# One slot order, several moves: PV ahead of the next pair's first V products, with their copy and sum at the end of the slot

## The chip, the cores and the metric

The kernel runs on 1 core of one Trainium2 chip. The metric is the device time of one execution in microseconds. It was 1584.73 us in the median of 3 runs (1584.5 to 1585.61). PE is TensorE, ACT ScalarE, DVE VectorE, POOL GpSimd, SP the engine that issues most DMAs. A layer of a transformer is computed: gated cross-attention, then a gated feed-forward network with ternary weights.

## The reference, cut to what matters

```python
# x, ctx: (8, 1024, 512); w_q, w_k, w_v: (512, 512); W1: (2048, 512); W2: (512, 2048)
q = layernorm(x) @ w_q;  k = ctx @ w_k;  v = ctx @ w_v
scores = where(causal, q @ k.T / sqrt(512), -inf)
x = x + tanh(g_xattn[0]) * softmax(scores) @ v
h = gelu(layernorm(x) @ ternary(W1).T + b1)          # exact gelu
x = x + tanh(g_ffn[0]) * (h @ ternary(W2).T + b2)
# ternary(w) = clip(round(w / mean|w|), -1, 1)
```

## The kernel before, in words

**Numbers.** Every float32 operand of an attention product is split into two float16 parts, an upper one (written by ACT) and a lower one (the rest, written by DVE). A product is three passes: upper*upper, lower*upper, upper*lower. Queries and keys are not formed: with A = w_q w_k^T, the scores are T ctx^T with T = layernorm(x) A.

**Attention, slots 1 to 64.** The 8192 rows of x are 64 tiles of 128 rows, 8 tiles to a batch. A slot t handles one tile, and each engine has its own `slot` function whose statements are its queue, in program order; an engine never passes a waiting instruction. In slot t PE does: the scores of tile t (L1704, into `s_ps`, as wide as (t mod 8 + 1) * 128 columns), the T product of a later tile (`t_product`, L1663), V products, and PV of tile t-1 (L1751, into `o_ps`, 3 * (t mod 8) products for t mod 8 > 0, else 24). DVE masks the scores (L1200), takes the maximum (L1202), the layer-norm statistics of the row tile five slots ahead (L1211 to L1134), the lower part of P (L1222), of T (`t_lower`, L1163), the normalised rows (`ln_rows`, L1140), V parts, and the update of `x_ring` from `o_ps` (L1266). ACT does the exponential (L773), the upper parts of P (L778), T (L788) and the rows (`rows_upper`, L796). POOL takes the power -1/2 (L563) and the lower part of the rows (L567). SP turns P, rows and loads by DMA.

**V by seven products.** From the third batch on V is made by pairs of 128 context rows: 24 pairs, u = 0 to 23, with a Strassen-like scheme of seven half-size products, each six matmuls of 256 columns (L1606). Pair u is spread over three slots. In the odd slot t = 13 + 2u (`pre`) PE does products 1 and 2 (`v_pre`, `v_part` 1 into `vp_a`, 2 into `vp_b`), ACT copies product 1 into `vr[:, 0]` (`v_first`, L733, first of three counts of `vr_out` for this pair), and DVE adds product 2 to it (`v11`, L1077). In the even slot t = 14 + 2u (`main`) PE starts the slot with product 6 (`v_six`, which waits for `v_first` of this pair, since it adds to the bank that `v_first` copies), then the scores, then product 5 (`v_five`, which waits for ACT's copy L740, `v_second`), T, and products 7 and 3; ACT and DVE finish three blocks (L751, L758, L1083, L1095, L1103). In the odd slot t = 15 + 2u (`tail`) PE does product 4 (`v_four`), DVE adds it (`v21`, L1089), ACT takes the upper part (`v21_upper`, L764) and DVE the lower (`v21_lower`, L1111). So an odd slot is tail of one pair and pre of the next. `v_second` of the next pair waits for `v21_lower`.

**Order in an odd slot before.** PE: scores, T, `v_four`, `v_pre`, PV. ACT: exponential and P, `t_upper`, `v_first`, `rows_upper`, `v21_upper`. DVE: mask and statistics, P, `t_lower`, `ln_rows`, `v21`, `v11`, `v21_lower`, then ternary weights in some slots, then the `x_ring` update.

**Last slots.** Slots 57 to 62 also start the feed-forward stage: `y_stats` and `y_normal` (L1315 to L1319, L1333) for the first rows, POOL's sums (L621 to L626) and lower parts (`y_lower`, L632), which `y_normal` of a later row waits for, and in slots 61 and 62 four `weight_sums` of two operations each (L1307), which the first unit's products wait for (`w1_sums`).

**Feed-forward, 64 units U of four blocks.** Seven products of W1 (L1510), GELU on ACT (L909), lower parts on DVE (L1359), and W2 (L1568). `add_bias` on POOL (L641) adds b2 to the rows of x, four at a time, in the units named in `BIAS`; the last ternary weights (L1405 to L1408) are made in units 0 to 2 of DVE.

Of the kernel before, what the change touches and what calls it, by code (L numbers as in the profile page):

```python
# [18 lines left out]
def gated_block(nc, x, ctxT, g_xattn, g_ffn, wqT, wkT, wv, w1T, b1c, w2T, b2, out):  # L19
# [4 lines left out]
    NT = N // P  # L24
# [3 lines left out]
    GT = 4  # L28
    NG = NT // GT
# [19 lines left out]
    with es:  # L49
# [141 lines left out]
        w_negs, w_ternary = sem("w_negs"), sem("w_ternary")  # L191
# [126 lines left out]
        def x2_first(e):  # L318

            g, i = e // GT, TILE[e % GT]  # L320
            if g:
                return x2_at(g, i)
            return (X2_SPARE, g32[:, 1], x_ring[:, 0], x_ring[:, 1])[e]

        def rows_step(g):

            return 0 if g == 1 else 4 * g - 5
# [1 line left out]
        EARLY = 6  # L329
        ROWS_Q0 = {rows_step(g): g for g in range(2, NG)}  # L330
        ROWS_Q1 = {0: 1, **{rows_step(g) + 1: g for g in range(2, NG)}}
        BIAS = {rows_step(g) + 2: g for g in range(1, NG)}

        def t_bank(s):

# [205 lines left out]
        def _(pool):  # L541
# [93 lines left out]
            def add_bias(e):  # L635

                x2 = x2_at(e // GT, TILE[e % GT])
                pool.wait_ge(y_rows, e + 1)
                if e == 0:
                    pool.wait_ge(vp_mm[4], NP)  # L640
                g.tensor_tensor(x2, x2_first(e), b2_row[:, :], ALU.add).then_inc(x2_biased, 1)  # L641

            def last_sum(U):
# [30 lines left out]

            last_sum(0)
            y_lower(2)
            for e in range(GT):
                add_bias(e)
            for U in range(NU):
                if U in ROWS_Q0:  # L680
                    y_scale(ROWS_Q0[U] * GT)
# [16 lines left out]
        def _(act):  # L698
# [29 lines left out]
            def v_first(u):  # L728

                act.wait_ge(vp_mm[1], u + 1)  # L730
                if u:
                    act.wait_ge(vb_split, nth_of(u - 1, BD_DONE))
                a.activation(vr[:, 0], vp_a, ACT.Copy).then_inc(vr_out, 1)  # L733
# [69 lines left out]
            def slot(it, s, last=False):  # L803
                t = it * BODY + s
                split, pre, main, tail = pair(t, SPLIT_AT), pair(t, PRE_AT), pair(t, MAIN_AT), pair(t, LAST_AT)
                if last and t == NT - 1:
                    unit_copy(0)
                if pre is not None:
                    ctx_parts_upper(pre)
                if main is not None:  # L810
                    v_second(main)
                    v_third(main)
                if not last or t < NT:
                    softmax(it, s)
                if not last or t < NT - T_LEAD:
                    t_upper(it, s)
                if pre is not None and pre:
                    v_first(pre)
                if not last or t + LN_LEAD < NT:
                    rows_upper(it, s)  # L820
                if t == 1:
                    ctx_upper(0, 0, 3)
                for q in FIRST_SPLITS.get(t, ()):
                    ctx_upper(1, 1, q)
                if t == 4:
                    weight_parts_upper()
                if t + 1 < PLAIN * TB:
                    v_upper(it, s)
                if pre == 0:
                    v_first(pre)  # L830
                if tail is not None:
                    v21_upper(tail)
                if main is not None:
                    v12_upper(main)
                    vd_upper(main)
                if split is not None:
                    b, q, par = pair_at(split)
                    ctx_upper(b, par, q)
                for m, n in w_turn(t, "S"):
                    sum_weight(m, n)  # L840
                if last and t in (FIRST_Y + 2, FIRST_Y + 4, FIRST_Y + 6):
                    y_upper((t - FIRST_Y) // 2 - 1)
# [125 lines left out]
        def _(dve):  # L968
# [218 lines left out]
            def slot(it, s, last=False):  # L1187
# [25 lines left out]
                    ln_variance(k, rk)  # L1213
                if pre is not None:
                    ctx_parts_lower(pre)
                if y_row is not None:
                    y_stats(y_row)
                if last and t == NT - 1:
                    unit_copy(0)
                if live:  # L1220
                    dve.wait_ge(p_hi, t + 1)
                    v.scalar_tensor_tensor(out=p_s[:, r, LO, 0:(i + 1) * P], in0=p32[:, 0:(i + 1) * P], scalar=P_UP,  # L1222
                                           in1=p_s[:, r, HI, 0:(i + 1) * P], op0=ALU.mult,
                                           op1=ALU.subtract).then_inc(p_split, 1)
                if not last or t < NT - T_LEAD:
                    t_lower(it, s)
                if norm:
                    ln_rows(k, rk, src, s + LN_LEAD >= 2)
                if tail is not None:
                    v21(tail)  # L1230
                if pre is not None:
                    v11(pre)
                if tail is not None:
                    v21_lower(tail)
                if main is not None:
                    v22(main)
                    v12_lower(main)
                    vd_lower(main)
                if t in (5, 6):
                    weight_parts_lower(t - 5)  # L1240
                if t + 1 < PLAIN * TB:
# [2 lines left out]
                    ternary(m, n, w_in[:, m % WR], w_loaded[m % WR], 16 * (m // WR + 1))  # L1244
                if last and t == NT - 1:
                    unit_first(0)
                if last and t == NT - 3:
                    weight_sums(0)
                    weight_sums(1)
                if last and t == NT - 2:  # L1250
                    weight_sums(2)
                    weight_sums(3)
                if last and t == NT:
                    unit_second(0)
                    lower(0, 0)
                if s >= 1:

                    q = (s - 1) % 2
                    v.reciprocal(rinv[:, q:q + 1], rowsum[:, q:q + 1]).then_inc(o_inv, 1)
                    dve.wait_ge(o_inv, t)  # L1260
                    par = ((s - 1) // TB) % 2
                    v.tensor_scalar(osc[:, q:q + 1], rinv[:, q:q + 1], fsc[:, par:par + 1], None,
                                    ALU.mult).then_inc(o_scaled, 1)
                    dve.wait_ge(o_scaled, t)
                    dve.wait_ge(pv_mm, t + PV0)
                    v.scalar_tensor_tensor(out=x_ring[:, (s - 1) % 8], in0=o_bank(last, s), scalar=osc[:, q:q + 1],  # L1266
                                           in1=x_ring[:, (s - 1) % 8], op0=ALU.mult, op1=ALU.add).then_inc(o_done, 1)
                if t == 1:
                    ctx_lower(0, 0, 3)
                for q in FIRST_SPLITS.get(t, ()):  # L1270
# [10 lines left out]
                if split is not None:  # L1281
                    b, q, par = pair_at(split)
                    ctx_lower(b, par, q)
                if y_row is not None:
                    y_normal(y_row)
                if t in TOTAL_SLOTS:
# [200 lines left out]
        def _(pe):  # L1487
# [198 lines left out]
            def slot(it, s, last=False):  # L1686
# [30 lines left out]
                    v_four(tail)  # L1717
                if t == PRE_AT:
                    v_product(it, s)
                if pre is not None:  # L1720
                    v_pre(pre)
                if last and t == NT:

                    unit_second(0)
# [10 lines left out]
                if s >= 1:  # L1735
# [13 lines left out]
                    for n, (pa, va) in enumerate(PASSES):  # L1749
                        for j in range(jn + 1):  # L1750
                            last_mm = mm(o_bank(last, s), pT[:, (s - 1) % 2, pa, j], v_s[:, par, va, j],  # L1751
                                         start=(n == 0 and j == 0), stop=(n == 2 and j == jn))
                    last_mm.then_inc(pv_mm, 1)

            pe.wait_ge(consts, 1)
            for _ in range(WARM):
# [75 lines left out]
```

## Time and profile before

| | |
|---|---|
| median of 3 runs | 1584.73 us |
| the profiled execution | 1584.63 us |
| its span, from first to last instruction | 1582.8 us |
| PE busy | 1554.9 us (98%) |
| DVE / ACT / POOL busy | 1165.2 / 871.8 / 590.3 us |
| granted PE clock over the span | 0.998 |

The span is what the trace covers; 1.83 us lie around it. A row of the timeline gives start and duration in us, engine, source line, operation, output and inputs, how many instructions were merged, and in brackets the idle time before it and who ended it. A row of the groups gives busy time, mean ns of one, and the idle time before them. Matmuls are pipelined: a product of 256 columns lasts 273 ns in the records, while six of them follow each other in 0.65 us, so the end of a merged PE row overlaps the next.

### The profile page before, as it was taken

The numbers are of one execution on the slowest core, as the hardware profiler recorded it, in microseconds if no ns is written. First come the engines' busy times: TensorE is split into PE (matmuls) and PEld (weight loads), VectorE is DVE, ScalarE is ACT, GpSimd is POOL, SyncE is SP. The second block draws the span as 40 slices with busy tenths as digits, with TensorE's granted clock in tenths as the row PEclk, the third lists the DMA queues.
The fourth block names the chain that finished last, engine by engine and source line by source line (L and its number), as shares of the span: only waits on it lengthen the run. The fifth ranks groups of instructions, "written<-read, shape, count | busy, mean of one in ns | idle before, by whom it ended". The sixth has DMA issues, their size and how long they took to land.

```text
span 1582.8 us, 27584 instructions
## 1 busy us (share of the span) xinstructions
PE 1554.9 (98%) x10456; PEld 1019.6 (64%) x10456; DVE 1165.2 (74%) x1973; ACT 871.8 (55%) x1575; POOL 590.3 (37%) x569
## 2 busy tenths in 40 slices
PE   8899999999999999998999999999999999999998
PEld 4556666676766666664666666666666666666665
DVE  6776678788988888876877667766766676767664
ACT  4344445544445444444666666666666666666654
POOL 5311223333324333243444444334534453445330
PEclk9999999999999999999999999999999999999999
DMA  7558657765656655553522333323332242224210
GB/s 213 140 104 196 149 139 185 150 145 137 146 132 144 150 130 132 134 141 85 127 77 78 66 82 82 83 72 65 93 83 78 49 101 77 77 48 100 51 51 27
DMA packets 310996, 170.91 MB, mean 108 GB/s; under 512 B 268544, under 2 KB 268560, under 8 KB 310608
## 3 DMA queue, kind: packets, MB, share of 16 engines
q1 hardware_dynamic: 309392, 166.52, 43.6%
q10 hardware_dynamic: 1296, 2.36, 0.4%
q8 instruction: 83, 1.36, 0.3%
q14 instruction: 49, 0.40, 0.1%
q0 software_dynamic: 176, 0.27, 0.1%
HBM read 70.53 MB, written 33.55 MB: 66 GB/s over the span
## 4 chain that ended last, share of the span: by engine, by line
PE 72%; DVE 16%; ACT 5%; issue 4%; DMA 1%; POOL 0%; SPq 0%; DVEq 0%; ACTq 0%
PE s_ps L1568 14%; PE e_ps L1568 13%; PE t_ps L1510 7%; PE v_ps L1510 7%; PE o_ps L1510 7%; PE o_ps L1751 6%; PE s_ps L1704 5%; PE t_ps L1663 5%; PE m_ps L1510 3%; PE e_ps L1606 2%; PE v_ps L1682 2%; DVE negmax L1202 2%; DVE ctx_s L989 2%; DVE x_ring L1266 1%; DVE xn_both L1140 1%
## 5 line engine op out<-in xcount | busy, mean ns | idle before, releaser
L1359 DVE SCALAR_TENSOR_TENSOR v_s<-xnT,sc,v_s 128x512 f16<-128x512 f32 x256 | 239.5, 956 | 105.7 <-ACT v_s L916 105.7
L909 ACT ACTIVATE xnT<-tT,b_s 128x256 f32<-128x256 f32 x384 | 174.0, 500 | 180.9 <-DVE tT L1347 64.8
L1568 PE MATMUL s_ps<-raw,v_s 128*128 128x512 f16 x1024 | 262.8, 379 | 0.8 <-DVE raw L1408 0.8
L1568 PE MATMUL e_ps<-raw,v_s 128*128 128x512 f16 x1024 | 262.8, 379 | 0.0
L1704 PE MATMUL s_ps<-ctx_s,tT 128*128 128x512 f16 (+3 forms) x1152 | 197.7, 326 | 4.7 <-DVE tT L1163 3.9
L1751 PE MATMUL o_ps<-v_s,pT 128*128 128x512 f16 x840 | 193.3, 381 | 3.5 <-DVE x_ring L1266 3.5
L916 ACT ACTIVATE v_s<-xnT,sc 128x512 f16<-128x512 f32 x256 | 176.2, 712 | 8.1 <-ACT xnT L909 0.8
L1568 PEld LDWEIGHTS e_ps<-raw,v_s 128*128 128x128 f16 x1024 | 100.2, 98 | 120.8
L647 POOL TENSOR_TENSOR tT<-tT 128x512 f32<-128x512 f32 x64 | 81.1, 1268 | 247.7 <-ACT tT L936 247.7
L1663 PE MATMUL t_ps<-xnT,a_s 128*128 128x256 f16 x1488 | 172.7, 273 | 0.1
L1704 PEld LDWEIGHTS s_ps<-ctx_s,tT 128*128 128x128 f16 x1152 | 105.5, 98 | 92.5 <-DVE tT L1163 5.9
L563 POOL TENSOR_TENSOR rstd<-var_s,minus_half 128x1 f32<-128x1 f32 x61 | 56.0, 919 | 291.7 <-DVE var_s L1134 291.7
L773 ACT ACTIVATE p<-s_ps,ebias,esc 128x128 f32<-128x128 f32 (+3 forms) x64 | 53.2, 831 | 194.4 <-DVE ebias L1206 194.4
L1663 PEld LDWEIGHTS t_ps<-xnT,a_s 128*128 128x128 f16 x1488 | 145.3, 98 | 21.0 <-DMA xnT<-xn_both 0.3
L1568 PEld LDWEIGHTS s_ps<-raw,v_s 128*128 128x128 f16 x1024 | 100.1, 98 | 68.1 <-issue 1.1
L1751 PEld LDWEIGHTS o_ps<-v_s,pT 128*128 128x128 f16 x840 | 82.5, 98 | 93.6 <-issue 6.1
L567 POOL TENSOR_TENSOR xn_both<-xn_both 128x512 f16<-128x512 f32 x61 | 71.1, 1166 | 150.0 <-ACT xn_both L796 150.0
L615 POOL TENSOR_TENSOR rstd<-var_s,minus_half 128x1 f32<-128x1 f32 x64 | 36.1, 565 | 218.8 <-DVE var_s L1319 218.8
L1341 DVE COPY tT<-t_ps 128x512 f32<-128x512 f32 x64 | 44.2, 691 | 85.0 <-PE t_ps L1510 85.0
L796 ACT ACTIVATE xn_both<-xn_both 128x512 f16<-128x512 f32 x64 | 40.3, 630 | 90.5 <-DVE xn_both L1140 90.0
L1353 DVE TENSOR_TENSOR tT<-tT,t_ps 128x512 f32<-128x512 f32 x64 | 44.0, 688 | 50.3 <-ACT tT L930 26.3
L641 POOL TENSOR_TENSOR v_work<-v_work,b_row 128x512 f32<-128x512 f32 x40 | 75.4, 1913 | 0.0
(232 smaller groups left out, 2831.2 us busy)
## 6 DMA issues: line engine op xcount, KB each, us to landing
out_y<-x_ring SPq DMA_DIRECT2D x128, 256.0 KB, 2.2
x_ring<-in_x SPq DMA_DIRECT2D x63, 256.0 KB, 2.9
raw<-in_ctxT SPq DMA_DIRECT2D x28, 512.0 KB, 4.0
v_work<-out_y SPq DMA_DIRECT2D x40, 256.0 KB, 3.9
w_in<-in_w1T SPq DMA_DIRECT2D x16, 512.0 KB, 3.8
w_in<-in_w2T SPq DMA_DIRECT2D x12, 512.0 KB, 3.9
x_ring<-out_y SPq DMA_DIRECT2D x22, 256.0 KB, 3.8
xnT<-xn_both SPq DMA_TRANSPOSE x128, 2.6
```

The costliest lines, as they stand in the source:

```text
L563: g.tensor_tensor(rstd[:, r:r + 1], var_s[:, r:r + 1], minus_half[:, :], ALU.pow).then_inc(ln_rstd, 1)
L567: g.tensor_tensor(xn_s[:, r, LO], xn32[:, r], xn_s[:, r, HI], ALU.subtract).then_inc(xn_lo, 1)
L641: g.tensor_tensor(x2, x2_first(e), b2_row[:, :], ALU.add).then_inc(x2_biased, 1)
L647: g.tensor_tensor(rr[:, R3], rr[:, R3], rr[:, R5], ALU.add).then_inc(c22_sum, 1)
L909: a.activation(g32n[:, j, half * 2 * P:(half + 1) * 2 * P], src, ACT.Gelu, bias=b1_s[:, f:f + 1], scale=1.0 / YN).then_inc(g_act, 1)
L916: a.activation(g_s[:, U % 2, j, HI], g32n[:, j], ACT.Copy, scale=col(C_SG)).then_inc(g_hi, 1)
L1359: v.scalar_tensor_tensor(out=g_s[:, U % 2, j, LO], in0=g32n[:, j], scalar=col(C_SG), in1=g_s[:, U % 2, j, HI], op0=ALU.mult, op1=ALU.subtr ...
L1510: last_mm = mm(bank[:, p * 2 * P:(p + 1) * 2 * P], w, yT[g % 2][:, a, row, c, :], start=(first and p == 0 and a == HI and c == 0), stop=(a ...
L1568: last_mm = mm(y_ps[i], g_s[:, U % 2, j, a, i * P:(i + 1) * P], w2_s[:, f, :], start=(U % UG == 0 and n == 0 and a == HI), stop=(U % UG == ...
L1663: last_mm = mm(bank[:, dd], a_s[:, aa, c, d * P:(d + 1) * P], xnT[:, pr, xa, c, :], start=(n == 0 and c == 0), stop=(n == 2 and c == DC - 1))
L1704: last_mm = mm(s_ps[:, lo:hi], tT[:, pr, ta, c, q * P:(q + 1) * P], ctx_s[:, par, ca, c, lo:hi], start=(n == 0 and c == 0), stop=(n == 2 a ...
L1751: last_mm = mm(o_bank(last, s), pT[:, (s - 1) % 2, pa, j], v_s[:, par, va, j], start=(n == 0 and j == 0), stop=(n == 2 and j == jn))
```

## The change

Nothing is computed otherwise; statements change their place in the queues. PE: `v_pre` goes behind PV. ACT: in the odd slot `v21_upper` goes ahead of `rows_upper`, and `v_first` to the end, behind `rows_upper` and (in even slots only) the context parts. DVE: `v21` goes ahead of `ln_rows`, `v11` behind the `x_ring` update; `y_stats` goes behind the V parts; the four `weight_sums` go from slots 61 (0, 1) and 62 (2, 3) to slot 62 (0, 1 in their old place, 2 behind the update) and slot 63 (3). POOL: the first four `add_bias` go from ahead of unit 0 to unit 2 and wait for the last ternary weights; those of group 1 go from unit 2 to unit 4.

```diff
@@ BIAS
-        BIAS = {rows_step(g) + 2: g for g in range(1, NG)}
+        BIAS = {2: 0, 4: 1, **{rows_step(g) + 2: g for g in range(2, NG)}}
@@ POOL, add_bias
                 if e == 0:
                     pool.wait_ge(vp_mm[4], NP)
+                    pool.wait_ge(w_ternary, NW)
@@ POOL, behind the slots
             y_lower(2)
-            for e in range(GT):
-                add_bias(e)
             for U in range(NU):
@@ ACT, slot
                     t_upper(it, s)
-                if pre is not None and pre:
-                    v_first(pre)
+                if tail is not None:
+                    v21_upper(tail)
                 if not last or t + LN_LEAD < NT:
                     rows_upper(it, s)
...
-                if pre == 0:
-                    v_first(pre)
-                if tail is not None:
-                    v21_upper(tail)
                 if main is not None:
                     v12_upper(main)
                     vd_upper(main)
                 if split is not None:
                     b, q, par = pair_at(split)
                     ctx_upper(b, par, q)
+                if pre is not None:
+                    v_first(pre)
@@ DVE, slot
-                if y_row is not None:
-                    y_stats(y_row)
                 if last and t == NT - 1:
                     unit_copy(0)
+                    weight_sums(3)
...
                     t_lower(it, s)
+                if tail is not None:
+                    v21(tail)
                 if norm:
                     ln_rows(k, rk, src, s + LN_LEAD >= 2)
-                if tail is not None:
-                    v21(tail)
-                if pre is not None:
-                    v11(pre)
                 if tail is not None:
                     v21_lower(tail)
                 if main is not None:
                     v22(main)
                     v12_lower(main)
                     vd_lower(main)
+                if y_row is not None:
+                    y_stats(y_row)
...
-                if last and t == NT - 3:
+                if last and t == NT - 2:
                     weight_sums(0)
                     weight_sums(1)
-                if last and t == NT - 2:
-                    weight_sums(2)
-                    weight_sums(3)
...
                                            in1=x_ring[:, (s - 1) % 8], op0=ALU.mult, op1=ALU.add).then_inc(o_done, 1)
+                if pre is not None:
+                    v11(pre)
...
                     ctx_lower(b, par, q)
+                if last and t == NT - 2:
+                    weight_sums(2)
                 if y_row is not None:
                     y_normal(y_row)
@@ PE, slot
-                if pre is not None:
-                    v_pre(pre)
...
                     last_mm.then_inc(pv_mm, 1)
+                if pre is not None:
+                    v_pre(pre)
```

## Rows read from the trace of the kernel before

**Rows 1.** Busy time in the pairs' slots; PE, PEld, DVE, ACT, POOL, clock, DMA.
```profile
187.00:691.00 504.00, 499.69 (x3541) 340.07 (x3538) 425.10 (x842) 233.35 (x433) 176.29 (x187) 1.00 0.60 142
```

**Rows 2.** Groups of PE instructions: products 6 and 5 of all pairs.
```profile
L1606 PE MATMUL e_ps<-v_work 128*128 128x256 f16 x432 | 59.0, 273 | 4.3 <-ACT vr L740 4.0
```

**Rows 3.** Timeline of slot 41 and the start of 42, odd-slot work.
```profile
...
496.35 0.38 ACT L733 ACTIVATE vr<-e_ps 128x256 f32<-128x256 f32 x1 [0.62 <-PE e_ps L1606]
...
496.56 0.68 DVE L1163 SCALAR_TENSOR_TENSOR tT<-t_ps,tT 128x512 f16<-128x512 f32 x1
...
497.16 0.54 DVE L1140 TENSOR_SCALAR xn_both<-x_ring,mv,rstd 128x512 f32<-128x512 f32 x1
...
497.45 0.82 PE L1606 MATMUL e_ps<-v_work 128*128 128x256 f16 x6
497.62 0.41 DVE L1089 TENSOR_TENSOR vr<-vr,e_ps 128x256 f32<-128x256 f32 x1
497.73 0.63 ACT L796 ACTIVATE xn_both<-xn_both 128x512 f16<-128x512 f32 x1 [1.00 <-DVE xn_both L1140]
...
498.70 1.17 DVE L1111 SCALAR_TENSOR_TENSOR v_s<-vr,v_s 128x256 f16<-128x256 f32 x1 [0.34 <-ACT v_s L764]
```

**Rows 4.** Timeline: the same two points of slots 43, 45 and 47.
```profile
514.83 0.68 DVE L1163 SCALAR_TENSOR_TENSOR tT<-t_ps,tT 128x512 f16<-128x512 f32 x1
...
515.41 0.82 PE L1606 MATMUL e_ps<-v_work 128*128 128x256 f16 x6
...
537.69 0.68 DVE L1163 SCALAR_TENSOR_TENSOR tT<-t_ps,tT 128x512 f16<-128x512 f32 x1
...
538.45 0.82 PE L1606 MATMUL e_ps<-v_work 128*128 128x256 f16 x6
...
564.71 0.68 DVE L1163 SCALAR_TENSOR_TENSOR tT<-t_ps,tT 128x512 f16<-128x512 f32 x1
...
566.41 0.82 PE L1606 MATMUL e_ps<-v_work 128*128 128x256 f16 x6
```

**Rows 5.** Timeline: end of T on PE, t_lower on DVE, slots 40, 42, 44.
```profile
484.42 0.82 PE L1606 MATMUL e_ps<-v_work 128*128 128x256 f16 x6
...
485.25 0.69 DVE L1163 SCALAR_TENSOR_TENSOR tT<-t_ps,tT 128x512 f16<-128x512 f32 x1 [0.38 <-ACT tT L788]
...
503.69 0.82 PE L1606 MATMUL e_ps<-v_work 128*128 128x256 f16 x6
...
505.03 0.69 DVE L1163 SCALAR_TENSOR_TENSOR tT<-t_ps,tT 128x512 f16<-128x512 f32 x1
...
522.61 0.39 PE L1577 MATMUL m_ps<-g,ones 128*128 128x128 f32 x2
...
524.86 0.68 DVE L1163 SCALAR_TENSOR_TENSOR tT<-t_ps,tT 128x512 f16<-128x512 f32 x1
```

**Rows 6.** Timeline of slots 61 to 64.
```profile
714.54 1.29 DVE L1307 TENSOR_TENSOR wv_s<-w_s 128x1024 f16<-128x1024 f16 x2
715.75 4.67 DVE L1307 TENSOR_TENSOR wv_s<-wv_s,w_s 128x1024 f16<-128x1024 f16 x2
715.83 4.03 POOL L632 TENSOR_TENSOR v_s<-v_s 128x1792 f16<-128x1792 f32 x1 [3.99 <-ACT v_s L860]
...
721.67 5.73 PE L1751 MATMUL o_ps<-v_s,pT 128*128 128x512 f16 x18 [3.51 <-DVE x_ring L1266]
...
732.62 0.30 DVE L1200 TENSOR_TENSOR s_ps<-s_ps,causal 128x128 f32<-128x128 f32 x1 [1.76 <-PE s_ps L1704]
...
742.78 5.35 PE L1751 MATMUL e_ps<-v_s,pT 128*128 128x512 f16 x24 [0.43 <-DMA pT<-p_s]
```

**Rows 7.** Timeline of the feed-forward units 1 and 2.
```profile
768.65 1.05 PE L1510 MATMUL t_ps<-ctx_s,a_s 128*128 128x256 f16 x8 [1.38 <-DVE tT L1341]
...
787.31 6.75 POOL L641 TENSOR_TENSOR v_work<-v_work,b_row 128x512 f32<-128x512 f32 x4
...
793.08 1.02 PE L1568 MATMUL s_ps<-raw,v_s 128*128 128x512 f16 x4 [0.82 <-DVE raw L1408]
```

## The prediction

> **What bounds the kernel now.** I read the busy times by stretch first. In the pairs' slots PE is busy 499.69 of 504 us [rows 1], and DVE 425: PE sets the pace, with DVE close behind, so what counts is each wait of PE. Then I read who ended PE's waits. In those slots the only ones of weight are product 5's waits for ACT's copy L740, 4.3 us of idle time [rows 2]; they stand in nine slots. The records hide part of each: a product of 256 columns lasts 273 ns [rows 2], but six follow each other in 0.65 us, so 0.16 of its record overlaps the next. The nine waits cost 4.3 + 9*0.16 = 5.8 us. Behind the pairs come a wait of 3.51 for DVE's `x_ring` update in slot 62 and one of 0.43 for P's DMA in slot 64 [rows 6], and 1.38 and 0.82 in units 1 and 2 [rows 7]. Nearly every us that an edit adds on PE's own path is a us of the kernel; one that it takes from DVE is worth something only at these waits.
>
> **What the reordering does to an odd slot.** Last I read the timeline of one odd slot and the start of the next [rows 3]. PE reaches product 6 at 497.45. ACT copied product 1 at 496.35, well before. The row copy L796 ran from 497.73 to 498.36, after PE had started product 6. Now L733 is put behind L796 on ACT, which never overtakes. So product 6, which needs L733, waits for a chain that nothing of PE waited for before. Moving `v_pre` behind PV leaves PE's arrival at product 6 where it was (the same work stands before it), and takes away the PV that lay between product 1 and product 6.
>
> The new chain, counted from the start of `t_lower`: L1163 to the next 0.60 (496.56 to 497.16), `v21` now first, with the 0.33 by which L1077 follows L1089 (0.41 busy, less the overlap of 0.08), rows L1140 0.54, hand-over 0.03 (497.70 to 497.73), row copy L796 0.63 less an overlap of 0.10 between neighbours on ACT, copy L733 0.38, hand-over to PE 0.06. Together 2.47 us. `v21_upper` fits beside the rows.
>
> Held against PE's arrival, if DVE kept its place:
> - slot 41: 496.56 + 2.47 = 499.03 against 497.45, 1.58 late [rows 3];
> - slot 43: 517.30 against 515.41, 1.89 late [rows 4];
> - slot 45: 540.16 against 538.45, 1.71 late [rows 4];
> - slot 47: 567.18 against 566.41, 0.77 late [rows 4].
> These four repeat in every batch.
>
> **What DVE gains back.** `v21_lower` L1111 took 1.17 and had 0.34 of idle time before it [rows 3]. It will start before POOL's work on the rows instead of beside it, and its ACT half will be ready: I take 0.42 and no wait, near the 0.41 of L1089, which has the same 256 columns (bounds 0.41 and 1.17). That is 1.1 us of DVE per odd slot, and PE comes later besides, so in the even slot DVE masks in time. There `t_lower` can't come sooner than T: 0.83 after T's end in slot 40 (484.42 to 485.25), where nothing held it. In slot 42 it came after 1.34, in slot 44 after 2.25 [rows 5]. So at most 0, 0.51 and 1.42 are won before slots 41, 43 and 45, and the rest of the even slot's DVE work follows as before. Slot 47 has a wider slot before it, with more DVE lateness to win; I take all of its 0.77.
>
> The waits at product 6: 1.58 in slots 17, 25, ... 57 (6 times, 9.5), 1.89 - 0.51 = 1.38 in slots 19, 27, ... 51 (5 times, 6.9), 1.71 - 1.42 = 0.3 in slots 21 ... 53 (5 times, 1.5), none in slots 23 ... 55. Sum 17.9. Bounds: with another 1.1 off each they sum to 6*0.48 + 5*0.28 = 4.3; no gain of DVE at all gives 6*1.58 + 5*1.89 + 5*1.71 + 5*0.77 = 31.3.
>
> On the other side all of the 5.8 at product 5 goes: `v21_lower`, which L740 waited for, ends over 1 us sooner, and PE comes later. Bounds 4 and 5.8. Net in the pairs' slots +12.1.
>
> **Slots 59 to 64.** Slot 59 has no row copy, but `v_first` stands behind `v21_upper`; its wait delays PE against a DVE that is late there anyway, so it is not added. The wait of 3.51 in slot 62 goes: no `weight_sums` stand before the update of slot 61. With it goes a slower stretch: 18 products took 5.73 where, at the (5.35 - 0.16)/24 = 0.216 of slot 64's, 18*0.216 + 0.16 = 4.05 would do [rows 6], 1.7 more. Worth 5.4. But who is late next? The second pair of L1307 took 4.67, the first 1.29, because POOL's L632, 4.03 long, lay across it [rows 6]. Now `y_normal` stands where that pair stood, and POOL's lower part comes no sooner, since it is queued behind a power that waits for the moved `y_stats`. I take DVE to be held till it ends, so that slot 62's mask comes about when it did. Ahead of the last mask DVE had 1.76 of idle time, so it was ready at 730.9 [rows 6]. Slot 62 now carries one pair of L1307 more, 1.3, and `y_stats`, which had stood in the shadow of ACT's P and now follows P: no row here, between 0.7 (one operation over 512 columns, as L1163's 0.68 [rows 3]) and 1.3; I take 1.0. The mask comes at 733.2, though PE has its scores 5.2 sooner, near 727.5. From that mask to the last PV, 732.62 to 742.78, is 10.16 [rows 6], a chain of DVE, ACT and DMA that PE's lead can't shorten: 743.4. So the last PV comes 0.6 later than it did, the wait moves from slot 62 to slot 64, 4 us or more, and the slow stretch behind a wait of that length comes again. I take +2.3 for this part (0.6 and 1.7). Bounds: -6.0, if DVE is held nowhere and the gain is kept (5.4, and 0.43 + 0.16 in slot 64), and +4.
>
> In the Trainium skill, SBUF — State Buffer, section Who interferes with whom, a VectorE operation with two SBUF inputs, or one in a 2-port mode as `tensor_scalar` may be, is fully blocked behind a GpSimd operation that reads SBUF. By that rule `y_normal` is held as the L1307 pair was, and the trace agrees for L1307 (4.67 beside 4.03). Were only two-input operations held, this part would give the lower bound.
>
> **Units 0 to 4.** Four `add_bias` ahead of unit 0 no longer lie beside DVE's work, and I take the 1.38 + 0.16 of unit 1 to go with them [rows 7]. Unit 2's 0.82 + 0.16 ends with a ternary operation beside POOL's 6.75 us of adds [rows 7]; the adds now wait for it. Gain 2.5. Bounds: 2.5, and a loss of 1 if the adds of units 2 and 4 hold DVE elsewhere. In slots 1 to 16 and from unit 5 on nothing on PE's path changes; the later groups of `add_bias` stand as they did.
>
> **Sum.** Against the profiled execution's 1584.63 (span 1582.8 and 1.83 around it, 0.1 below the median of 1584.73): +17.9 - 5.8 + 2.3 - 2.5 = +11.9, 1596.5.
>
> **Rivals.**
> *The tail keeps its gain.* DVE is not held in slot 61, the last mask is on time: -6.0 instead of +2.3, 1588.2. For it: DVE had 1.76 of idle time before that mask. Against it: the amount of work moved there.
> *Faster: DVE's lead is carried through.* The 1.1 us per odd slot that L1111 and its wait give back comes off the chain of the next odd slot in full. The waits at product 6 sum to 4.3, which the 5.8 at product 5 pays; with the tail's 6.0 and the units' 2.5 the time is 1574.6. It decides once the waits at product 6 sum to less than 14.3 with the tail kept. Against it: in slot 40 `t_lower` followed T as soon as it could [rows 5], so there is nothing to be won before slot 41.
> *The late copy doesn't bind.* PE doesn't wait at product 6 at all, since the rows are done by then: -5.8 + 2.3 - 2.5, 1578.6. Against it: L796 ended 0.9 after product 6 had started [rows 3].
> *DVE wins nothing for the odd slots.* Another operation meets POOL's work in place of L1111, and masks stay as late as before: +31.3 - 5.8 + 2.3 - 2.5, 1609.9.
>
> **How the numbers follow.** Forecast 0.64, within 1591 to 1601; the tail's gain kept 0.12; DVE's lead 0.07; copy not binding 0.03; nothing won 0.12; 0.02 for neither. About 0.2% (3.2 us) is what a measurement of this kernel tells from no change. The tail rival straddles that bound: half same, half slower. So faster 0.1, same 0.07, slower 0.83. The range runs from the tail rival's lower half to midway to the worst case: 1585 to 1603.
>
> **What would show it.** Right: PE waits at L1606 for L733, some 17 times, 1.4 to 1.6 in slots 1 and 3 of a batch; L740 is gone as its releaser; L1111 falls to 0.4; the largest single PE wait is at the last PV, for pT, and none for the `x_ring` update; no PE wait in units 1 and 2. Wrong: PE's idle time in the pairs' slots stays under 8 us, or the last mask follows the last scores at once.

## The result and the profile after

The changed kernel took 1596.23 us in the median (1594.69 to 1597.79), the one before 1584.63 (1584.5 to 1585.61) beside it: the ratio is 1.0072, interval 1.0057 to 1.0088. The change makes the kernel slower by 0.72%, 11.6 us; the forecast was +11.9.

The page of the profile after. Its execution was the longest one, 1597.79 us, so 1.6 over the median:

```profile
span 1596.0 us, 27584 instructions
PE 1557.7 (98%) x10456; PEld 1019.2 (64%) x10456; DVE 1150.5 (72%) x1973; ACT 874.6 (55%) x1575; POOL 586.2 (37%) x569
```

DVE gave back 14.7 us of work, and the span still grew by 13.2. The busy times of the pairs' slots, the same stretch as [rows 1] (columns: stretch, its length, then PE, weight loads, DVE, ACT, POOL, granted clock, DMA share, GB/s):

```profile
187.00:691.00 504.00, 489.25 (x3453) 330.44 (x3452) 400.68 (x820) 230.92 (x424) 167.37 (x181) 1.00 0.61 140
```

PE's idle time grew from 4.3 to 14.75 us at an unchanged clock. The chief waits of PE by who ended them (total, times, longest):

```profile
PE e_ps L1603 <- ACT vr L732: 16.4, 17, 1.7
PE s_ps L1492 <- DMA ctx_s<-in_wqT: 3.4, 2, 2.6
PE e_ps L1660 <- DMA xnT<-xn_both: 3.4, 1, 3.4
PE s_ps L1701 <- DVE tT L1160: 2.9, 3, 1.9
PE v_ps L1507 <- ACT tT L927: 2.4, 1, 2.4
PE s_ps L1701 <- ACT p L772: 1.8, 2, 1.0
```

And the groups that answer to [rows 2] (L1606 is L1603 now) and to the 1.17 of L1111 in [rows 3] (the second is the view of that line by itself: min, median and longest duration in ns):

```profile
L1603 PE MATMUL e_ps<-v_work 128*128 128x256 f16 x432 | 59.1, 273 | 16.4 <-ACT vr L732 16.4
```
```profile
L1108 DVE SCALAR_TENSOR_TENSOR v_s<-vr,v_s x24: 424/425/426, 218.8 to 729.7; 128x256 f16<-128x256 f32 x24
```

Product 5's wait for ACT's second copy is gone, and 17 waits for the first copy (L732, L733 before) stand in its place. One of them step by step, the end of slot 41 and the start of slot 42, against [rows 3]:

```profile
504.36 0.82 PE L1603 MATMUL e_ps<-v_work,ctx_s 128*128 128x256 f16 x6
505.01 0.81 PE L1746 MATMUL o_ps<-v_s,pT 128*128 128x512 f16 x3
505.66 0.82 PE L1603 MATMUL e_ps<-wv_s,ctx_s 128*128 128x256 f16 x6
506.08 0.68 DVE L1160 SCALAR_TENSOR_TENSOR tT<-t_ps,tT 128x512 f16<-128x512 f32 x1
506.31 0.82 PE L1603 MATMUL v_ps<-wv_s,ctx_s 128*128 128x256 f16 x6
506.68 0.41 DVE L1086 TENSOR_TENSOR vr<-vr,e_ps 128x256 f32<-128x256 f32 x1
507.01 0.54 DVE L1137 TENSOR_SCALAR xn_both<-x_ring,mv,rstd 128x512 f32<-128x512 f32 x1
507.12 0.42 ACT L763 ACTIVATE v_s<-vr 128x256 f16<-128x256 f32 x1 [1.87 <-DVE vr L1086]
507.57 0.42 DVE L1108 SCALAR_TENSOR_TENSOR v_s<-vr,v_s 128x256 f16<-128x256 f32 x1
507.58 0.63 ACT L795 ACTIVATE xn_both<-xn_both 128x512 f16<-128x512 f32 x1
508.12 0.37 ACT L732 ACTIVATE vr<-e_ps 128x256 f32<-128x256 f32 x1
508.29 1.16 POOL L567 TENSOR_TENSOR xn_both<-xn_both 128x512 f16<-128x512 f32 x1 [2.06 <-ACT xn_both L795]
508.54 0.83 PE L1603 MATMUL e_ps<-v_work 128*128 128x256 f16 x6 [1.41 <-ACT vr L732]
```

Read it from the bottom. PE starts product 6 at 508.54, when the copy at 508.12 is done. The copy stood behind the rows' copy (507.58) on ACT, that behind `ln_rows` on DVE (507.01), that behind `v21` (506.68) and `t_lower` (506.08). Yet ACT had been idle for 1.87 us ahead of 507.12, and the product that it copies ended with the six products of 505.66. PE waits for a queue's order, not for data or for work.

The last slots, against [rows 6] (the first row is where slot 60's scores start):

```profile
707.59 3.42 PE L1701 MATMUL s_ps<-ctx_s,tT 128*128 128x512 f16 x24
...
731.75 3.59 POOL L632 TENSOR_TENSOR v_s<-v_s 128x1792 f16<-128x1792 f32 x1
732.17 3.44 DVE L1330 TENSOR_SCALAR w_in<-v_work,mv,rstd 128x512 f32<-128x512 f32 x1
735.54 0.29 DVE L1197 TENSOR_TENSOR s_ps<-s_ps,causal 128x128 f32<-128x128 f32 x1
738.57 5.34 PE L1701 MATMUL s_ps<-ctx_s,tT 128*128 128x512 f16 x24 [1.01 <-ACT p L772]
...
746.65 0.29 DVE L1197 TENSOR_TENSOR s_ps<-s_ps,causal 128x128 f32<-128x128 f32 x1
...
752.47 1.28 ACT L906 ACT_TABLE_LOAD   x1
755.21 1.05 PE L1507 MATMUL v_ps<-ctx_s,a_s 128*128 128x256 f16 x8 [2.40 <-ACT tT L927]
756.81 6.82 PE L1746 MATMUL e_ps<-v_s,pT 128*128 128x512 f16 x24 [0.55 <-DMA pT<-p_s]
```

`y_normal` (L1330) is held for 3.44 us beside POOL's 3.59; one such operation that is held nowhere takes 0.54, as L1137 above. In the program this `y_normal` waits for no count of that lower part, so it isn't a semaphore that holds it. The wait of 3.51 for `x_ring` is gone. In the stretch behind 756.7 the granted clock falls to 0.61, as it fell to 0.57 behind the wait of 3.51 before:

```profile
756.70:760.70 4.00, 3.89 (x12) 1.50 (x13) 1.04 (x3) 2.79 (x6) 2.58 (x2) 0.61 0.02 7
```

### The profile page after: what moved, and what is told of

Read it like the earlier page. It is cut to its first block, busy times and chain, and to the rows that moved or that the text cites. A ratio compares the mean times of both kernels' runs of the same rounds, so it can differ in the third digit from the quotient of the medians.

```text
span 1596.0 us, 27584 instructions
## 1 busy us (share of the span) xinstructions
PE 1557.7 (98%) x10456; PEld 1019.2 (64%) x10456; DVE 1150.5 (72%) x1973; ACT 874.6 (55%) x1575; POOL 586.2 (37%) x569
## 3 DMA queue, kind: packets, MB, share of 16 engines
q8 instruction: 83, 1.36, 0.4%
## 4 chain that ended last, share of the span: by engine, by line
PE 76%; DVE 14%; ACT 4%; issue 3%; DMA 1%; POOL 1%; SPq 0%; DVEq 0%; ACTq 0%
PE s_ps L1565 14%; PE e_ps L1565 14%; PE s_ps L1701 7%; PE o_ps L1507 7%; PE t_ps L1507 7%; PE v_ps L1507 7%; PE o_ps L1746 6%; PE t_ps L1660 5%; PE m_ps L1507 3%; PE e_ps L1603 3%; PE v_ps L1679 2%; DVE ctx_s L986 2%; DVE negmax L1199 1%; DVE v_work L1065 1%; DVE x_ring L1259 1%
## 5 line engine op out<-in xcount | busy, mean ns | idle before, releaser
L1603 PE MATMUL e_ps<-v_work 128*128 128x256 f16 x432 | 59.1, 273 | 16.4 <-ACT vr L732 16.4
```

The source lines that it names most:

```text
L1603: last_mm = mm(bank, left(ca, c), right(va, c), start=(first and n == 0 and c == 0), stop=(n == 2 and c == 1), skip_group_check=True)
```

## Experiments

Each ratio is against the kernel before, run on the same chip in the same rounds (its medians were 1585.29, 1585.95 and 1585.39 in the three groups of runs), with its 95% interval. Two theories stood against each other. Theory A: the late place of `v_first` on ACT makes PE wait, and the other moves help or are nothing. Theory B: PV's place ahead of `v_pre`, or the moves of the last slots, cost the time.

### The copy early, the products ahead of PV, and each part by itself

**e1_copy_early**, the change with one call moved on ACT:

```diff
                     t_upper(it, s)
+                if pre is not None:
+                    v_first(pre)
                 if tail is not None:
                     v21_upper(tail)
...
-                if pre is not None:
-                    v_first(pre)
                 for m, n in w_turn(t, "S"):
```

> The changed kernel with one statement moved: ACT's copy of product 1 stands directly behind the upper part of T, ahead of v21_upper and of the row copy; PV stays ahead of products 1 and 2. My theory (product 6 waits only because its copy is queued behind the rows, which wait for DVE): the 17 waits at product 6, 19.2 us in the changed kernel's profile, fall under 2 us in all, since the copy needs 0.38 and product 2 runs 0.65 beside it. The product-5 waits of the old kernel don't come back, since v21_lower stays early. Time 1596.2 - 17.5 = 1578.7, within 1577 to 1581, and faster than the kernel before. Rival A (the nearness of product 1 to product 6, now that PV no longer lies between them, is what costs): a wait of 0.4 or more stays in each of 23 slots, and the rows come later behind a copy that waits for PV: 1588 or more. Rival B (the rest of the change, DVE's order or the last slots, carries the loss): 1594 or more.

1579.22 us (1578.0 to 1580.18), ratio 0.9961 [0.9948, 0.9973]. One call's place turns the change from 0.7% slower to 0.4% faster, 17 us. In its trace, the same group and the same stretch as above:

```profile
L1603 PE MATMUL e_ps<-v_work 128*128 128x256 f16 x432 | 59.0, 273 | 1.5 <-ACT vr L739 1.3 <-ACT vr L732 0.3
187.00:691.00 504.00, 502.49 (x3564) 340.96 (x3563) 412.74 (x850) 238.24 (x441) 175.11 (x190) 1.00 0.61 143
```

The 16.4 us are 0.3, and PE is idle for 1.51 of 504 us. Against the expectation, 1.3 us of product 5's waits (for L739) came back, in two slots.

**e2_products_before_pv**, the change with PE's move undone:

```diff
                     v_product(it, s)
+                if pre is not None:
+                    v_pre(pre)
                 if last and t == NT:
...
                     last_mm.then_inc(pv_mm, 1)
-                if pre is not None:
-                    v_pre(pre)
```

> The changed kernel with PE's move undone: products 1 and 2 stand ahead of PV again, ACT and DVE as changed. My theory: the wait at product 6 ends with the copy behind the rows, whose chain starts at t_lower; PE's order inside the slot changes neither that chain nor PE's arrival at product 6. So the waits stay at 19 us, 1.5 in slots 1 and 1.4 in slots 3 of a batch, and the time at 1596 (1594.5 to 1598). Rival A (the place of PV): the waits go, 1578 to 1582.

1595.78 (1594.15 to 1596.2), 1.0064 [1.0052, 1.0077]: no different from the change. The waits didn't move either:

```profile
PE e_ps L1603 <- ACT vr L732: 16.5, 17, 1.7
```

PV's place costs nothing here, and theory B's first half falls. The traces say it more sharply than the times: from slot 0's first score product to the last product of the program the change takes 1548.94 us and e2 1549.01. It also shows that product 1 is early enough in either place.

**e3_only_copy_late**, the kernel before with the late copy alone:

```diff
                     t_upper(it, s)
-                if pre is not None and pre:
-                    v_first(pre)
                 if not last or t + LN_LEAD < NT:
                     rows_upper(it, s)
...
-                if pre == 0:
+                if pre is not None:
                     v_first(pre)
                 if tail is not None:
                     v21_upper(tail)
```

> The kernel before with one statement moved: ACT's copy of product 1 stands behind the row copy, ahead of v21_upper. My theory: the chain from t_lower to product 6 is 2.47 less the 0.33 of v21, 2.14 us, so product 6 is late by 1.25 in slots 1 and by 1.56 less 0.5 in slots 3 of a batch, and by about 0.2 in slots 5: 6*1.25 + 5*1.1 + 5*0.2 = 14. Product 5 waits less, but not in the narrow first slot of a batch, since DVE's v11 now waits for the copy ahead of v21_lower: 2 of its 5.8 go. Time 1584.6 + 14 - 2 = 1596.6, within 1592 to 1600: this one move alone costs what the whole change costs. Rival B (the loss comes from DVE's order, PE's order or the last slots): 1583.5 to 1587.

1593.26 (1591.05 to 1594.89), 1.0051 [1.0038, 1.0065]. One move by itself costs 8 us. It came out 3.3 below the value expected, though inside the range: the waits in slots 1 and 3 of a batch are shorter than I had them (slot 1: 1.11 to 1.24), apart from slot 57's 2.19, slot 5 has none, and all of product 5's went. So a PE that comes later is enough to hide product 5's copy, with `v21_lower` as late as before.

```profile
PE e_ps L1604 <- ACT vr L733: 11.3, 11, 2.0
```

11.3 and 11 * 0.17 hidden in the records make 13.2, less the 5.8 of product 5: 7.4. A wait for T in slot 60, 0.66 and its hidden part, went with them: 6.6, and the two traces differ by 6.5 from slot 0's first score product on. The change has the longer waits since there `v21` comes ahead of `ln_rows` too: the 0.33 that the prediction counted for it is the difference in each of ten slots (1.44 to 1.57 in slot 1 of a batch, against 1.11 to 1.24 here).

**e10_copy_between**, the change with the copy halfway, behind `v21_upper` and ahead of `rows_upper`:

```diff
                     v21_upper(tail)
+                if pre is not None:
+                    v_first(pre)
                 if not last or t + LN_LEAD < NT:
...
-                if pre is not None:
-                    v_first(pre)
```

> The changed kernel with ACT's copy of product 1 between v21_upper and the row copy. My theory gives the length of the chain for this place as well: from the start of t_lower 0.60, v21 0.41, hand-over 0.04, v21_upper 0.40 less 0.10, copy 0.38, hand-over 0.06, together 1.79 instead of 2.47, 0.68 shorter. So the 17 waits of 1.5, 1.35 and 0.33 become about 0.85 six times, 0.65 five times and none, 1.2 in slot 59: 9.5 less than in the changed kernel, 1596.2 - 9.5 = 1586.7, within 1585 to 1589, halfway to the early copy's 1579.2. Rival D (it is the row copy as such that holds ACT, so anything ahead of it is free): 1579 to 1581.

1587.43 (1584.32 to 1589.69), 1.0012 [1.0003, 1.0021].

```profile
PE e_ps L1603 <- ACT vr L732: 8.3, 12, 1.7
```

Behind the rows 1596.23, ahead of them 1587.43, ahead of `v21_upper` as well 1579.22: the time follows the copy's place step by step. Slot 1 of a batch waits 0.77 to 0.91 here and slot 3 0.56 to 0.71, as the chain with the rows' terms taken off gives. Slot 59 still waits 1.88, where 1.2 was expected: no row copy stands in it, so this move changes nothing there. No run came near rival D's 1579 to 1581 (the fastest took 1584.32). Theory A stands.

**e15_only_third_block_early**, the kernel before with only the third block moved, the copy staying first:

```diff
@@ ACT
                     v_first(pre)
+                if tail is not None:
+                    v21_upper(tail)
                 if not last or t + LN_LEAD < NT:
...
-                if tail is not None:
-                    v21_upper(tail)
@@ DVE
                     t_lower(it, s)
-                if norm:
-                    ln_rows(k, rk, src, s + LN_LEAD >= 2)
                 if tail is not None:
                     v21(tail)
+                if norm:
+                    ln_rows(k, rk, src, s + LN_LEAD >= 2)
```

> The kernel before with v21 ahead of ln_rows on DVE and v21_upper ahead of the row copy on ACT, v_first staying ahead of both: the part of the change that I take to be its gain. My theory: v21_lower runs before POOL's rows work, 0.42 instead of 1.17, and the nine waits at product 5, 5.8 us, go down to 0 to 1; nothing waits at product 6; the last slots keep their waits. 1585.5 - 5.3 = 1580.2, within 1579 to 1582. Rival (that time is given back at the next wait, DVE being close behind): 1584 or more.

1581.37 (1577.51 to 1582.74), 0.9972 [0.996, 0.9983]. This is the part of the change that pays in the pairs' slots. L1111 takes 0.42 in all 24 slots, and of product 5's 4.3 us nothing is left; the 0.3 is a wait at product 6 in slot 57:

```profile
L1606 PE MATMUL e_ps<-v_work 128*128 128x256 f16 x432 | 58.9, 273 | 0.3 <-ACT vr L733 0.3
```

### The last slots and the units

**e4_last_slots_undone**, the change with `y_stats` and the `weight_sums` back in their old places:

```diff
+                if y_row is not None:
+                    y_stats(y_row)
                 if last and t == NT - 1:
                     unit_copy(0)
-                    weight_sums(3)
...
-                if y_row is not None:
-                    y_stats(y_row)
...
-                if last and t == NT - 2:
+                if last and t == NT - 3:
                     weight_sums(0)
                     weight_sums(1)
+                if last and t == NT - 2:
+                    weight_sums(2)
+                    weight_sums(3)
...
-                if last and t == NT - 2:
-                    weight_sums(2)
```

> The changed kernel with y_stats and the four weight_sums in their old places. My theory: the wait of 3.5 us for the x_ring update in slot 62 and its slow stretch come back and the waits in slot 64 go, since the last mask is the same chain either way; y_stats ahead of P costs 1 us at product 6 in slot 57. Net between -1 and +2, 1596.8. Rival (those moves keep their gain of 5.4, and something else in the last slots costs): 1601 or more.

1593.23 (1592.77 to 1596.95), 1.0057 [1.0044, 1.007]. That is 2.0 below the lower end of what was expected. By the ratios the moves of the last slots cost 0.15% in the change, 2.4 us, but the intervals of the two overlap. In the trace the `x_ring` wait is back, and this time no slow stretch follows it: 18 products took 5.73 there before [rows 6] and take 4.04 here. Nor does one follow the wait of 0.41 at the last PV. But one stands earlier: slot 57's wait at product 6 is 2.35, 1.0 longer than in the change, as expected of `y_stats`, and behind it the granted clock of 4 us is 0.57.

```profile
686.67 0.99 PE L1603 MATMUL e_ps<-v_work 128*128 128x256 f16 x6 [2.35 <-ACT vr L732]
...
736.73 4.04 PE L1746 MATMUL o_ps<-v_s,pT 128*128 128x512 f16 x18 [2.88 <-DVE x_ring L1261]
...
756.13 5.35 PE L1746 MATMUL e_ps<-v_s,pT 128*128 128x512 f16 x24 [0.41 <-DMA pT<-p_s]
```
```profile
687.00:691.00 4.00, 4.00 (x18) 2.10 (x16) 1.50 (x3) 0.38 (x1) 3.92 (x6) 0.57 0.43 116
```

So of what the change removed and brought back, 1.7 us and 1.5 are the clock behind a wait, which is not at the same wait in every trace. From slot 0's first score product on, e4's trace is only 0.4 us shorter than the change's; that the moves of the last slots cost anything is not shown.

**e11_early_row_late**, e1 with slot 61's `y_normal` put behind the next slot's mask:

```diff
                                     ALU.mult).then_inc(s_bias, 1)
+                if y_row == 5:
+                    y_normal(4)
                 if norm:
...
-                if y_row is not None:
+                if y_row is not None and y_row != 4:
                     y_normal(y_row)
```

> The kernel with the early copy (1579.2 us), and DVE's normalising of the fifth feed-forward row moved from the end of slot 61 behind the mask and bias of slot 62. My theory: that operation is what lies 3.44 us behind POOL's lower part and makes the mask of slot 62 about 1.9 late; the mask reads PSUM and isn't held by POOL. Moved behind it, the wait of 1.2 for the exponential in slot 63 goes, and the chain to the last PV starts up to 1.8 sooner: 1577.4, within 1576.5 to 1579. Rival (the last PV is set by POOL's and ACT's rows work anyway): 1579.2.

1577.7 (1575.84 to 1578.86), 0.9948 [0.9936, 0.9961], which overlaps e1's interval. The order of DVE beside POOL's lower part:

```profile
714.74 3.59 POOL L632 TENSOR_TENSOR v_s<-v_s 128x1792 f16<-128x1792 f32 x1
716.70 0.30 DVE L1197 TENSOR_TENSOR s_ps<-s_ps,causal 128x128 f32<-128x128 f32 x1 [1.46 <-PE s_ps L1703]
717.03 1.09 DVE L1199 TENSOR_REDUCE negmax<-s_ps 128x1 f32<-128x896 f32 x1
718.29 0.54 DVE L1332 TENSOR_SCALAR w_in<-v_work,mv,rstd 128x512 f32<-128x512 f32 x1
```

The mask and the maximum, which read PSUM, run at their usual length in the middle of POOL's operation; `y_normal` now starts as that operation ends (718.29 against 718.33) and takes 0.54 instead of 3.44. PE's wait of 1.0 for the exponential is gone. From slot 60's scores to the end of the last PV the trace is 2.8 us shorter than e1's: 1.1 are waits, and 1.7 a fall of the clock that e1's trace has and this one has not.

**e12_early_row_late_stats_early**, e11 with `y_stats` back ahead of P's lower part:

```diff
                     ctx_parts_lower(pre)
+                if y_row is not None:
+                    y_stats(y_row)
...
-                if y_row is not None:
-                    y_stats(y_row)
```

> As the one before, and y_stats back ahead of P's lower part, where DVE waits for ACT in slots 60 to 62. My theory: 1.0 us of DVE goes back into that shadow in each of slots 60, 61 and 62, and the last mask, late against PE's scores, comes 1 sooner in slot 62; in slots 57 to 59 it stands ahead of P and can cost up to 1. Net 0 to -1 against it: 1576.8, within 1575.5 to 1578. Rival (y_stats ahead of P costs more in slots 57 to 59 than it gives): 1578.5 or more.

1576.06 (1575.09 to 1577.58), 0.9938 [0.9925, 0.9952]. It lies in the range expected, but its interval overlaps e11's. In the traces it loses 1.1 us against e11 up to slot 60's scores and wins 2.4 from there to the end of the last PV.

**e9_early_bias_undone**, e1 with the `add_bias` moves undone:

```diff
-        BIAS = {2: 0, 4: 1, **{rows_step(g) + 2: g for g in range(2, NG)}}
+        BIAS = {rows_step(g) + 2: g for g in range(1, NG)}
...
-                    pool.wait_ge(w_ternary, NW)
...
             y_lower(2)
+            for e in range(GT):
+                add_bias(e)
```

> The kernel with the early copy (1579.2 us), and the adds of b2 back ahead of unit 0 and in unit 2. My theory: the waits of 1.5 for DVE's copy in unit 1 and of 1.0 for the ternary weights in unit 2 come back, 2.3 net of the 0.25 that is left now: 1581.5, within 1580.5 to 1582.5. Rival (DVE catches up there, the waits are paid back later): 1579.

1580.35 (1579.63 to 1582.8), 0.9968 [0.9956, 0.9981], against 0.9961 of e1, and just below the range expected. The waits of units 1 and 2 are back in the trace (1.32 and 0.98 with the hidden parts, against 0.25 in the change), but in time only 1.1 us shows, inside both intervals. That these moves win 2 us rests on the traces, not on a timed difference.

### The best version

**e6_early_products_before_pv** is e1 with `v_pre` ahead of PV again, **e13_best_products_before_pv** is e12 with the same edit:

```diff
                     v_product(it, s)
+                if pre is not None:
+                    v_pre(pre)
...
-                if pre is not None:
-                    v_pre(pre)
```

> The kernel with ACT's copy of product 1 directly behind the upper part of T (1579.2 us), and besides that products 1 and 2 ahead of PV again. My theory: once the copy is early, PV's place is off PE's path: products 1 and 2 and PV take the same time in either order, and the 0.38 of the copy is hidden beside product 2 or beside PV. Same time, 1578 to 1580.5. Rival A (PV ahead costs something by itself, the copy and its hand-over just behind product 1): faster by 2 or more, under 1577. Rival C (PV ahead is what frees DVE's x_ring update and so pays): 1582 or more.

1577.85 (1577.12 to 1579.57), 0.9951 [0.9938, 0.9963]. With the copy early neither product 5 nor product 6 waits any more, and PE fills the whole stretch:

```profile
L1603 PE MATMUL e_ps<-v_work 128*128 128x256 f16 x432 | 58.9, 273 | 0.0
187.00:691.00 504.00, 504.00 (x3578) 343.66 (x3576) 414.09 (x853) 237.56 (x439) 175.82 (x191) 1.00 0.62 143
```

The 0.10% to e1 is within both intervals, so the times alone don't tell the two apart. The traces do: from slot 0's first score product to slot 60's, e6 takes 645.91 us and e1 647.97. The 2.06 are e1's two waits for L739 and the one for L732, with their hidden parts. So beside the early copy `v_pre` ahead of PV is worth 2 us in the trace, while beside the late copy (e2) it was worth nothing. The expectation had it off PE's path.

> The fastest kernel so far (1576.1: early copy, fifth row behind the mask, y_stats ahead of P) with products 1 and 2 ahead of PV again. My theory: as beside the early copy alone, where it was 1577.9 against 1579.2 and the last waits at products 5 and 6 (2.1 us) were gone from the profile: 1574.5, within 1573 to 1576. Rival (that difference was scatter): 1576.

1574.59 (1572.99 to 1574.77), 0.9929 [0.9917, 0.9941]: the fastest here, 0.7% ahead of the kernel before and 1.4% ahead of the change. The interval overlaps e12's again, and the traces again give 2.0 us up to slot 60's scores (647.20 against 649.23). It keeps of the change the third block ahead of the rows, `v11` behind the update, the spread `weight_sums` and the late `add_bias`, and has `v_first` and `y_stats` early.

## Why the prediction was right

The time (1596.23 against 1596.5) and the cause are as predicted, and so is the sign; two terms were off against each other: slot 59's wait, left out, and the last slots, put too high. The traces sum to 10 where I had 11.9, so the mechanism is shown, but a forecast within 0.3 us of the median is luck. Durations below are from starts to starts, with the part that the records hide.

- **The chain.** 2.47 us were counted from `t_lower` to product 6. In slot 41 it is 506.08 to 508.54, 2.46.
- **The waits at product 6.** Slot 1 of a batch: 1.44 to 1.57 against 1.58, 9.1 in all against 9.5. Slot 3: 1.22 to 1.36 against 1.38, 6.6 against 6.9. Slot 5: 0.33 five times, 1.65 against 1.5. Slot 7: none, as said. Sum 17.4 against 17.9. That DVE's gain reaches back only as far as T lets it, the argument on slots 40, 42 and 44 [rows 5], is what sized these; with no gain it would have been 31.3.
- **Product 5.** All 5.8 gone. Both reasons given hold: `v21_lower` ends sooner (L1108 took 0.42, the value taken), and PE comes later; by e15 and e3 either is enough alone.
- **Slot 59.** I left its wait out, as delaying PE against a DVE that is late anyway. It is 1.87 us.
- **Slots 60 to 64.** `y_normal` is held behind POOL, the mechanism forecast. The Trainium skill, SBUF — State Buffer, section Who interferes with whom, names `tensor_scalar` as an operation that can block on GpSimd; by that rule, the trace agrees (3.44 against 3.59). It says as well that an operation with one SBUF input outside those modes doesn't contend, and the mask and maximum from PSUM in e11 agree. From slot 60's scores to the last PV PE loses 6.5 us in the changed kernel against 7.6 before; with slot 59 it is 8.4. So +0.8 stands where I had +2.3. What I mis-sized is the mask of slot 62, which I took to come when it did: it comes 2.1 us sooner, 27.95 behind slot 60's scores against 30.09 (the rows below, and 735.54 against 707.59 above). DVE's update of `x_ring` now starts ahead of POOL's operation (L1259 at 731.51 against 731.75), where before it came behind it (L1266 at 720.77, POOL's end at 719.86). The detail was wrong too: I had the one large wait at the last PV, for pT. The last mask came at 746.65 and the last PV 10.16 later, to the hundredth as before; but the 4 us of waiting fell apart into 0.53, 1.17, 2.57 and 0.72 at four places. The largest is at a product ahead of the last PV, which needs a bank that ACT copies (L927) behind P, a copy of rows, a table load of 1.28 and the first GELU. It would have been seen by asking, for each product of PE in the last slot, whose bank it overwrites.
- **Units 0 to 4.** 2.3 gained in the trace, 2.5 forecast.

The start of slot 60's scores and the mask of slot 62 in the kernel before:

```profile
691.80 3.43 PE L1704 MATMUL s_ps<-ctx_s,tT 128*128 128x512 f16 x24 [0.66 <-DVE tT L1163]
...
721.89 0.29 DVE L1200 TENSOR_TENSOR s_ps<-s_ps,causal 128x128 f32<-128x128 f32 x1
```

By the traces this sums to 17.4 - 5.8 + 0.8 - 2.3 = +10.1. The profiled execution came out 13.16 above the one before, and 3.25 of it lie ahead of slot 0's first score product, where no edit is (the first row is of the kernel before, the second of the changed one):

```profile
39.35 0.83 PE L1704 MATMUL s_ps<-ctx_s,tT 128*128 128x128 f16 x12
```
```profile
42.60 0.83 PE L1701 MATMUL s_ps<-ctx_s,tT 128*128 128x128 f16 x12
```

PE waits 3.4 there for the first weights (L1492, 0.8 before); in e2's trace, of the same head, that wait is 0.2. From this product to the last one of the program the traces differ by 9.94, so the account leaves nothing open between them. The medians are 11.6 apart, 1.6 more. Each trace is one execution: over the 13 traces the head ends between 39.16 and 42.60, and each fall of the clock behind a wait adds about 1.5 us or more. The 34 executions of the kernel before beside the experiments have medians of 1585.29 to 1585.95, and from these the change is 10.3 to 10.9 away. Why e4's waits from slot 61 on cost 3.6 us where those of the change cost 5.0 stays open; these are single traces of each.

The rivals: that the late copy doesn't bind fell by e1 and e10. That DVE wins nothing for the odd slots fell with slot 3 and slot 5 of the batches. That DVE's lead is carried through fell, since it can't pass T. That the tail keeps its gain fell as stated, +0.8 instead of -6.0.

## What to carry to other kernels

On an in-order engine the copy that frees or fills a bank for the bottleneck engine belongs where its input is ready, ahead of anything that waits for a slower chain: here its place alone, with the same work, was worth 17 us, 1.1%. Size such a wait by adding the chain from the last point that can't move, and let a lead won upstream count only as far as that point lets it. Bundled moves are to be timed one by one: one of these lost 17 us beside the others (8 by itself) and hid others that, without it, win 6. And a move that was worth nothing beside a wait (`v_pre` in e2) can be worth something once that wait is gone (2 us in e6's trace).

## What was not expected of the hardware

- Behind PE's wait of 3.51 [rows 6] and behind 2.40 and 0.55 in a row in the change, the granted clock fell to 0.57 and 0.61 of the 4 us that follow, near the lower of its two levels (1.2 against 2.4 GHz) for some 3 us, which cost 1.7 and 1.5 us. The last PV's 24 products took 6.82 for it, against 5.35 in e4. Behind e4's wait of 2.88 it stayed at full speed, though it fell behind the 2.35 of slot 57 in the same trace. In e15 the fall behind 3.51 lasted longer: the 18 products took 6.89, 2.8 us more than the 4.05 of the change. The clearest case is the scores of slot 62, where e1 and e6 both waited 2.00 for T: in e6 the clock fell and the 24 products took 1.7 us longer, in e1 it didn't. A wait of two to three microseconds can cost half as much again and more, its length doesn't settle whether it does, and two single traces can differ by this alone.

The 4 us from such a wait's end, the clock third from the end of the row, in the kernel before and in e4:

```profile
721.60:725.60 4.00, 3.93 (x11) 1.51 (x12) 2.83 (x7) 1.97 (x3) 0.55 (x1) 0.57 0.87 185
```
```profile
736.70:740.70 4.00, 3.97 (x19) 1.86 (x20) 2.78 (x7) 2.02 (x3) 0.55 (x1) 1.00 0.87 187
```

The scores of slot 62 in e1 and in e6:

```profile
711.82 4.71 PE L1701 MATMUL s_ps<-ctx_s,tT 128*128 128x512 f16 x24 [2.00 <-DVE tT L1160]
```
```profile
710.52 6.40 PE L1701 MATMUL s_ps<-ctx_s,tT 128*128 128x512 f16 x24 [2.00 <-DVE tT L1160]
```

- A `tensor_scalar` of 512 columns, SBUF to SBUF, was held for all of POOL's operation, 3.44 instead of 0.54, though it has a single tensor input; started as that operation ended, it took 0.54. What reads PSUM went through beside it.
